# One-hots of a second batch on ScalarE, 0.2 t by a second broadcast, later negatives of x, and bent rows in other pieces, in a graph-attention kernel on one core

## What is computed

```python
HW = h @ W
s = HW @ a[:OUT_F, 0];  t = HW @ a[OUT_F:, 0]
e = leaky_relu(s[row] + t[col], negative_slope=0.2)
m = segment_max(e, row);  ex = exp(e - m[row])
att = ex / segment_sum(ex, row)[row]
agg = segment_sum(att[:, None] * h[col], row)
out = silu(agg) @ base_w.T + einsum('nip,oip->no', b_splines(agg), spline_w)
x = layernorm(x + out)
```

## Time and profile before

| | |
|---|---|
| median of 3 runs | 391.12 us (391.08 to 391.19) |
| the profiled execution's own time | 391.19 us |
| its span in the profile | 389.4 us |
| PE busy | 374.6 us (96%) |
| VectorE busy | 342.1 us (88%) |
| ScalarE busy | 254.7 us (65%) |
| granted TensorE clock, mean | 0.999 |

### The profile page before, as it was taken

One profiled execution on the slowest core, in us unless ns is written; L12 is line 12 of the kernel. 1 busy time (PEld: TensorE's weight loads), 2 busy tenths in 40 slices (PEclk: granted clock), 3 DMA queues, 4 the chain that ended last, 5 costly groups with the idle time before them and its releaser, 6 DMA issues.

```text
span 389.4 us, 5102 instructions
## 1 busy us (share of the span) xinstructions
PE 374.6 (96%) x1915; PEld 299.1 (77%) x1915; DVE 342.1 (88%) x428; ACT 254.7 (65%) x248; POOL 35.9 (9%) x89
## 2 busy tenths in 40 slices
PE   6899889999999999999999999999999999999994
PEld 3556557888888888788888888888888888888883
DVE  8999999987775698999899999889999899989255
ACT  6879643454446979784878764868668686865222
POOL 6001210000000010010100101010010101001000
PEclk9999999999999999999999999999999999999999
DMA  7905970000000055368565553724332554723202
GB/s 253 397 16 125 204 220 2 1 0 2 0 2 0 2 186 193 113 187 267 163 166 158 147 174 120 209 55 108 109 96 66 158 160 116 248 69 99 66 27 101
DMA packets 23634, 46.56 MB, mean 120 GB/s; under 512 B 1882, under 2 KB 2098, under 8 KB 23610
## 3 DMA queue, kind: packets, MB, share of 16 engines
q0 software_dynamic: 12400, 24.00, 24.0%
q1 hardware_dynamic: 11210, 22.25, 17.2%
HBM read 43.67 MB, written 2.57 MB: 119 GB/s over the span
## 4 chain that ended last, share of the span: by engine, by line
PE 85%; DVE 11%; issue 2%; POOL 1%; DVEq 0%; ACT 0%; POOLq 0%
PE PS L1269 63%; PE PS L1212 18%; DVE oh L450 5%; DVE still L464 3%; PE PS L1194 3%; PE PS L1222 1%; DVE scrap L624 0%; DVE ex L640 0%; ACT ex L952 0%; DVE st L832 0%; DVE xr L827 0%; DVEq L247 0%; DVE xr L848 0%; DVE mk L501 0%; DVE C L672 0%
## 5 line engine op out<-in xcount | busy, mean ns | idle before, releaser
L1269 PE MATMUL PS<-wh,s 128*128 128x512 f32 x720 | 223.0, 390 | 0.4 <-issue 0.4
L1269 PEld LDWEIGHTS PS<-wh,s 128*128 128x128 f32 x720 | 135.1, 188 | 29.8 <-issue 1.9
L1269 PE MATMUL PS<-wl,s 128*128 128x512 f32 x360 | 140.1, 389 | 0.0
L1269 PEld LDWEIGHTS PS<-wl,s 128*128 128x128 f32 x360 | 67.6, 188 | 14.0
L1008 ACT ACTIVATE s<-v 128x1280 fp32r<-128x1280 f32 (+1 forms) x32 | 40.0, 1251 | 41.9 <-DVE v L810 23.4
L991 ACT ACTIVATE v<-xt,bias 128x1280 f32<-128x1280 f32 (+1 forms) x32 | 42.9, 1340 | 18.9 <-DVE s L820 17.6
L804 DVE SCALAR_TENSOR_TENSOR v<-v,v 128x1280 f32<-128x1280 f32 (+1 forms) x32 | 46.4, 1451 | 6.3 <-ACT v L994 6.3
L810 DVE SCALAR_TENSOR_TENSOR v<-v,v 128x1280 f32<-128x1280 f32 (+1 forms) x32 | 46.7, 1461 | 3.7 <-DVE v L806 0.5
L820 DVE SCALAR_TENSOR_TENSOR s<-v,s 128x1280 fp32r<-128x1280 f32 (+1 forms) x32 | 46.5, 1454 | 3.3 <-ACT s L1008 3.3
L439 POOL DMA_DIRECT2D wh<-in_splT x32 | 23.0, 717 | 269.9 <-PE PS L1269 172.0
L806 DVE SCALAR_TENSOR_TENSOR v<-v,v 128x1280 f32<-128x1280 f32 (+1 forms) x32 | 46.5, 1453 | 0.0
(11 more groups left out here) (148 smaller groups left out, 332.5 us busy)
## 6 DMA issues: line engine op xcount, KB each, us to landing
wh<-in_splT POOLq DMA_DIRECT2D x32, 512.0 KB, 4.1
wring<-in_splT SPq DMA_DIRECT2D x21, 512.0 KB, 3.9
xt<-in_xT SPq DMA_DIRECT2D x1, 2500.0 KB, 11.9
xh<-in_x POOLq DMA_DIRECT2D x1, 2304.0 KB, 12.3
out<-xr SPq DMA_DIRECT2D x9, 256.0 KB
wh<-in_baseT POOLq DMA_DIRECT2D x4, 512.0 KB, 5.4
xl<-in_x POOLq DMA_DIRECT2D x1, 1536.0 KB, 11.8
wring<-in_baseT SPq DMA_DIRECT2D x3, 512.0 KB, 4.6
```

The lines of the kernel that those rows point to most:

```text
L1269: m = e.matmul(PS[:, w % 8, :], sx[:, ic, tl * 128:tl * 128 + 128], wx[:, ic, :], start=first and n == 0, stop=last and n == 2)
```

## The change

1. Batch 12's `oh` is made by ScalarE: two absolute differences (of 2*REACH[12] = 316 columns) after the copies of each of batches 4 to 7, into two arrays of their own, and a relu over four tiles (1264 columns) after batches 8 and 9. VectorE skips that comparison but keeps its wait for the ring.
2. `st_rows` also writes 0.2 times the rows; SP stores both rows and issues a second broadcast (to `gentle`) behind the first. ScalarE's multiplication at L1024 is gone.
3. The negatives of x are at batches 8 to 17 instead of 6 to 15.
4. `most_along` and what follows it on VectorE come one batch earlier.
5. `bent` of row block 0 has three pieces (0 to 512, 512 to 880, 880 to 1250); the first moves into the middle of the loop body, the second is at its end. The first 500 columns of row block 1's `bent` stand ahead of `weigh(0, 0)`, the other 750 at the old place.

```diff
-BY_SCALAR = 3
+BY_SCALAR, BY_TOO = 3, 12
-HALF = 512
+HALF, NEXT, BEGUN = 512, 880, 500
-        ENDS_AT, MOST_AT, SIZES_AT = 6, 9, NB - 1
-        NEGATIVE_AT = {6 + k: k for k in range(NT)}
+        ENDS_AT, MOST_AT, SIZES_AT = 6, 8, NB - 1
+        NEGATIVE_AT = {8 + k: k for k in range(NT)}
+        DIFFERENCES_AT, ONES_AT = (4, 5, 6, 7), (8, 9)
...
-            e.wait_ge(s_srow, 1)
+            e.wait_ge(s_srow, 2)
             for k, (lo, hi) in enumerate(TCH):
-                e.dma_start(t_row[0:1, lo:hi], strow[32 * k + 1:32 * k + 2, 0:hi - lo]).then_inc(s_tline, 16)
+                e.dma_start(t_row[:, lo:hi].unsqueeze(0), strow[32 * k + 1:32 * k + 2, :, 0:hi - lo]).then_inc(s_tline, 16)
             e.wait_ge(s_tline, 64)
             e.dma_start(trow[:, :], t_row[0:1, :].partition_broadcast(128)).then_inc(s_trow, 16)
+            e.dma_start(gentle[:, :], t_row[1:2, 0:N].partition_broadcast(128)).then_inc(s_gentle, 16)
...
             def moving(b):
-                if b == BY_SCALAR:
+                if b >= RB:
+                    e.wait_ge(s_ct, done(b - RB))
+                if b in (BY_SCALAR, BY_TOO):
                     return
                 h = REACH[b]
-                if b >= RB:
-                    e.wait_ge(s_ct, done(b - RB))
...
-                if b == ENDS_AT + 3:
+                if b == ENDS_AT + 2:
                     most_of_tiles()
...
                     marks(MARKED, ND, 0, NEAR).then_inc(s_near, 1)
+                    bent(0, 0, HALF).then_inc(s_first, 1)
                     e.wait_ge(s_early, n + 1)
...
                     e.tensor_tensor(top[:, 0:LW], trow[:, d], Z[:, 0, d], ALU.subtract).then_inc(s_touch, 1)
-                    bent(0, 0).then_inc(s_first, 1)
+                    bent(0, HALF, NEXT).then_inc(s_next, 1)
...
             greatest(0)
             small(0)
-            bent(0, 1).then_inc(s_z, 1)
+            e.wait_ge(s_next, left)
+            bent(0, NEXT, N).then_inc(s_z, 1)
+            bent(1, 0, BEGUN).then_inc(s_begun, 1)
             weigh(0, 0)
             weigh(0, 1)
             greatest(1)
-            bent(1).then_inc(s_z, 1)
+            e.wait_ge(s_begun, 1)
+            bent(1, BEGUN, N).then_inc(s_z, 1)
...
+            def differences(t):
+                h = REACH[BY_TOO]
+                return e.activation(off_too[t // 4][:, t % 4, :], im[:, MV // 2 - h:MV // 2 + h], ACT.Abs,
+                                    bias=mk_by[:, 1, t:t + 1], scale=-1.0).then_inc(s_off, 1)
+            def ones_of(part):
+                h, k = REACH[BY_TOO], TB // 2
+                e.wait_ge(s_ct, done(BY_TOO - RB))
+                e.wait_ge(s_off, 2 + k * part + k)
+                e.activation(oh[:, BY_TOO % RB, part * k:part * k + k, 0:2 * h], off_too[part][:, :, :], ACT.Relu, bias=1.0,
+                             scale=-1.0).then_inc(s_by, 1)
             def st_rows():
                 e.wait_ge(s_sr, 1)
-                e.copy(strow[0:98, :], PS[0:98, 6, 0:384]).then_inc(s_srow, 1)
+                e.copy(strow[0:98, 0, :], PS[0:98, 6, 0:384]).then_inc(s_srow, 1)
+                e.mul(strow[0:98, 1, :], PS[0:98, 6, 0:384], SLOPE).then_inc(s_srow, 1)
...
+                if b in DIFFERENCES_AT:
+                    differences(2 * DIFFERENCES_AT.index(b))
+                    differences(2 * DIFFERENCES_AT.index(b) + 1)
+                if b in ONES_AT:
+                    ones_of(ONES_AT.index(b))
...
-            e.wait_ge(s_trow, 16)
-            e.mul(gentle[:, :], trow[:, 0:N], SLOPE).then_inc(s_gentle, 1)
...
+                elif b == BY_TOO:
+                    e.wait_ge(s_by, 4)
                 else:
-                    e.wait_ge(s_mv, b + (b < BY_SCALAR))
+                    e.wait_ge(s_mv, b + 1 - (b > BY_SCALAR) - (b > BY_TOO))
```

More of the change, by code:

```diff
@@ L164, in build @@
         dn = at("dn", 33, [128, 2, 128], I32)
+        off_too = [at(f"off{k}", 34 + k, [128, TB // 2, 2 * REACH[BY_TOO]], F16) for k in range(2)]
         war = at("war", 33, [128, 128], F32, 2048)
-        strow = at("strow", 32, [128, 384])
+        strow = at("strow", 32, [128, 2, 384])
         left_col, left_sq, left_in, reach_col = (at(f"left{k}", 36, [128, NCP], F32, 704 * k) for k in range(4))
@@ L193, in build @@
         s_setup = sem("s_setup")
-        (s_reach, s_bits, s_col, s_mk, s_bound, s_left, s_tab, s_mv, s_head, s_ovk, s_ovm, s_ovs, s_ova, s_ovz, s_marked, s_early, s_near, s_touch, s_first, s_late, s_tmax, s_small, s_z, s_p, s_den, s_rden, s_plo,
+        (s_reach, s_bits, s_col, s_mk, s_bound, s_left, s_tab, s_mv, s_head, s_ovk, s_ovm, s_ovs, s_ova, s_ovz, s_marked, s_early, s_near, s_touch, s_first, s_next, s_begun, s_late, s_tmax, s_small, s_z, s_p, s_den, s_rden, s_plo,
          s_a3, s_b3, s_spl, s_slo, s_wlo, s_res, s_bns, s_bna, s_rstd, s_nb, s_fin) = (
             sem(f"v_{n}") for n in (
-                "reach", "bits", "col", "mk", "bound", "left", "tab", "mv", "head", "ovk", "ovm", "ovs", "ova", "ovz", "marked", "early", "near", "touch", "first", "late", "tmax", "small", "z", "p", "den", "rden", "plo",
+                "reach", "bits", "col", "mk", "bound", "left", "tab", "mv", "head", "ovk", "ovm", "ovs", "ova", "ovz", "marked", "early", "near", "touch", "first", "next", "begun", "late", "tmax", "small", "z", "p", "den", "rden", "plo",
                 "a3", "b3", "spl", "slo", "wlo", "res", "bns", "bna", "rstd", "nb", "fin"))
@@ L630, in marks, with bent @@
                 return e.tensor_scalar(Z[:, j0:j1, d], C[:, j0:j1, d], 0.0, BIG, ALU.is_equal, ALU.mult)
-            def bent(j, p=0):
-                lo, hi = pieces(j)[p]
+            def bent(j, lo, hi):
                 if j >= 3:
@@ L764, in _ @@
             greatest(2)
-            bent(2).then_inc(s_z, 1)
+            bent(2, 0, N).then_inc(s_z, 1)
             small(2)
@@ L772, in _ @@
             greatest(3)
-            bent(3).then_inc(s_z, 1)
+            bent(3, 0, N).then_inc(s_z, 1)
             small(3)
@@ L779, in _ @@
             inverse(3)
-            bent(4).then_inc(s_z, 1)
+            bent(4, 0, N).then_inc(s_z, 1)
             greatest(5)
@@ L785, in _ @@
                 if j + 3 < NT:
-                    bent(j + 3).then_inc(s_z, 1)
+                    bent(j + 3, 0, N).then_inc(s_z, 1)
                 if j + 2 < NT:
@@ L887, in moving_by_scalar @@
                 e.wait_ge(s_mk, 1)
-                e.copy(mk_by[:, :], mk[:, TB * b:TB * b + TB, 0]).then_inc(s_by_mk, 1)
+                apart = TB * (BY_TOO - b)
+                e.copy(mk_by[:, :, :], mk[:, TB * b:TB * b + 2 * apart, 0].rearrange("p (a k) -> p a k", a=2)[:, :, 0:TB]
+                       ).then_inc(s_by_mk, 1)
                 e.wait_ge(s_by_mk, 1)
@@ L894, in moving_by_scalar @@
                         m = e.activation(off[:, t, :], im[:, MV // 2 - h:MV // 2 + h], ACT.Abs,
-                                         bias=mk_by[:, part * k + t:part * k + t + 1], scale=-1.0)
+                                         bias=mk_by[:, 0, part * k + t:part * k + t + 1], scale=-1.0)
                     m.then_inc(s_off, 1)
```

8 lines of the change are left out of this document (4 added, 4 removed).

## The result

The changed kernel takes 392.69 us, median of 6 runs (392.55 to 393.43), beside 391.15 us (391.08 to 391.23) for the kernel before on the same chip: ratio 1.0044, 95% interval 1.0033 to 1.0056. It is slower, by 1.5 us; the forecast was 390.1 us, and its range ended at 391.7 us.

A forecast was written before the change was run, and what follows sets the result against it. VectorE's pace, then a short VectorE and ScalarE chain, bounds the kernel before 53.59 us, TensorE afterwards. Terms of -1.22 us plus 0.2 us for xl's wait gave -1.0 us, so 390.1 us, range 389.6 to 391.7.

The forecast's parts named there:

- The views and the bound: Whole kernel: before 53.59 us each microsecond won moves the end, if nothing holds TensorE afterwards; cheaper work behind wins nothing.
- Part 1: Batch 12's one-hot comparison leaves VectorE and TensorE can follow: -1.39 us.
- Part 2: ScalarE's bill for batch 12 and the second row copy: 6.7 us more work, cost 0, bound +0.4 us.
- the eight differences fit into the waits: ScalarE up to the pair copied at 22.82 us: batch 12's added differences cost only idle time.
- Part 3: 0.2 t by DMA through a second broadcast on SP's queue: cost 0, with 6 us of cover before VectorE's need.
- Part 4: VectorE's bent in pieces: +0.35 us in the loop, -0.08 at its end, -0.10 after small.
- Part 5: Negatives of x two batches later delay GpSimd's adding loads of xl, using up 5.6 us of slack: +0.2 us wait.
- When the stream starts: GpSimd's first adding load of xl is issued at 37.4 us, 4.5 us later than before.
- How long it runs: Adding stream moves by 4.5 us to land at 54.2, or 53.5 with up to 0.7 us back from a gone broadcast.
- The weights: SP's 1.05 MB of wring, issued with about 3 us of adding stream left, should not hold xl: 0.
- turn by turn: Rival, 15%: wring and xl packets alternate between two queues, adding 1.7 us to xl's landing; likeliest 391.3 us.
- the clock: TensorE ahead of the sums: a wait of a microsecond or two would not lower its granted clock; no chance assigned.

The follow-up runs named there:

- o_no12: Batch 12's comparison back on VectorE, against the changed kernel with row block 0's xl products last (389.37 us): 389.86 us, 0.9966 of the kernel before.
- o_most9: MOST_AT 9 again (most_along one batch later), against the changed kernel with row block 0's xl products last (389.37 us): 388.49 us, 0.9933 of the kernel before.
- x_gact: Changed kernel without the second broadcast: ScalarE computes gentle from trow again, bent in its old pieces; 393.72 us, 1.0058 of the kernel before.
- x_neg6: Changed kernel with the negatives of x back at batches 6 to 15, xl products at their old place; 395.83 us, 1.0124 of the kernel before.
- o_bent_back: bent back in its old pieces, against the changed kernel with row block 0's xl products last (389.37 us): 389.48 us, 0.996 of the kernel before.
- x_warm: Changed kernel with thirteen products with nought filling TensorE's wait ahead of the xl products; 392.51 us, 1.0032 of the kernel before.
- the control: Changed kernel with only two more register operations on VectorE, which all variants hold; 393.69 us, 1.0072 of the kernel before.
- b_neg8: The kernel before with only the negatives of x moved two batches later, to start at batch 8; 391.20 us, 0.9999 of the kernel before.
- x_loads_again: Changed kernel with SyncE's and GpSimd's first weight loads both waiting for all of xl, run once more for a second profile; 391.08 us, one run.
- x_wring_after_xl: Changed kernel with only SyncE's wring loads waiting for xl, GpSimd's wh load still released by tmax; 391.18 us, 1.0003 of the kernel before.

## Why the prediction was wrong

**The views and the bound** were right: before 53.59 us a microsecond is a microsecond, provided nothing holds TensorE after it. That proviso failed.

**Part 1 (-1.39)** was right for the front. The still of batch 20 came at 42.90 us for 44.97, 2.07 earlier, and at 44.30 in `o_no12`, so part 1 by itself is worth 1.40. The other 0.67 are luck: an idle 0.58 us ahead of batch 19's comparison that I had not priced. In the chain of before a load of a register from `r_size` (2.2 us) stands ahead of it. Without part 1 that load still took 2.5 us, but the earlier `MOST_AT` started it 1.8 us sooner and the idle time was gone (`o_no12`); with part 1 and the old `MOST_AT` it took 0.84 us and the idle time was gone too (`o_most9`). Either is enough. Why the load is short with part 1 was not found.

**Part 2 (0, bound +0.4)**: the prices were a little high (from start to start a difference of 316 columns takes 0.45 us and a relu 1.15, for 0.48 and 1.25), and there was no wait from 23 to 44 us. The step "the eight differences fit into the waits" was right only for an early start. They used up all of ScalarE's idle time after the second pair of copies, and a late start of it is no longer absorbed: a wait of VectorE's of 0.25 us in the profiled execution, and of 0 to 1.18 us over the variants. That is beyond the bound of 0.4, and no term of the sum had it.

**Part 3 (0)**: right in its price; `x_gact` found none for the second broadcast. The landings were 2 us later than reckoned, `trow` 34.61 + 4.2 = 38.8 us for 36.7 and `gentle` 40.4 for 38.4, with cover enough. I had not seen that the two broadcasts stand in the way of an earlier adding stream, which `x_neg6` shows.

**Part 4 (+0.35, -0.08, -0.10)**: right, +0.34, -0.16 and -0.11 by the same distances in the two traces. `o_bent_back` cannot tell its 0.1 us from noise. Sum of parts 1 to 4: forecast -1.22, measured -1.76: -2.07 for the stills, +0.25 for the wait at the marks and +0.07 for part 4, to 0.01.

**Part 5** is the step that failed. *When the stream starts* was right (37.50 for 37.4). *How long it runs* was one sample taken for a constant: I took the 16.8 us of one trace, or up to 0.7 less, and streams alone take 16.8 to 18.4. The 0.7 rested on "that is gone", said of a broadcast ahead of the stream, and it was not gone: SyncE's queue still moved 58 packets in 39 to 40 us, when the stream had its first. *The weights*: I read the 163 packets to 18 as "the load that came first was served nearly alone" and set this to 0. That held until past 52 us and then no longer: the queues shared, and it cost 1.2 to 1.6 us. The trace of before had it one microsecond further on, while the last 0.14 MB of GpSimd's load were still to come. Its queues in 190 to 191 us:

```profile
q1 hardware_dynamic: 149, 0.31, 82.5%
q0 software_dynamic: 52, 0.09, 27.8%
```

The rival "turn by turn" (15%) had the mechanism, with 1.7 us for it, but from the moment of the issue; by the Trainium skill (DMA: Bandwidth & Descriptors, Queues, rings and completion order) the engines alternate packet by packet, and from 53 us on the trace agrees, 75 to 82; from 51 to 52 us it does not, 98 to none.

And the rival's own sum, 391.3 us, was still 1.4 short, because of *the clock*. I wrote that a wait of a microsecond or two "does not frighten me", from a stretch in which TensorE was busy for 0.69 of a microsecond. The wait was 2.81 us of full idleness, the clock went to 1.2 GHz, and 1.7 us were lost on top of it: 6.44 us for twenty products that take 4.84 in `x_warm`, where TensorE was kept busy. The time of `x_warm` is 1.2 us below the control's.

So the slack of 5.6 us that part 5 used "to the microsecond" was spent from three sides: the stream 4.6 us later, its reader 1.8 us earlier through the gain itself, the transfer beside it 1.6 us earlier through that same gain. The first, 3.6 us of it, is free alone, by `b_neg8`; the other two were not tried without it.

## What to carry to other kernels

A gain at the front brings forward whatever it releases: ask of each transfer that it triggers which other one is still under way, and whose reader is now earlier too. Idle time that is filled with moved work no longer absorbs a late start, as on ScalarE here: with the `xl` products last, the three kernels with part 1 scatter by 0.8 to 1.3 us and the one without it by 0.06. Slack that a forecast uses up entirely is a risk on one side only, since a wait of a few microseconds on TensorE also costs its clock; put the work that needs the late operand last, as here, where this order gives 389.37 us, 0.9945 (0.9932 to 0.9958) of the kernel before, and with `MOST_AT` at 9 388.49, 0.9933 (0.9919 to 0.9946), the lowest median, which the intervals do not tell apart. And two queues seen 163 to 18 in one microsecond say who came first, not who will be served next: read the microseconds after it as well.

## What the runs showed of the hardware that was not expected

SyncE's load got its first packets between 3.5 and 4.5 us after its issue (48.50 us, 52 to 53 us) while GpSimd's adding stream was saturated, and an equal share from 53 us on. With no other queue busy such a load had its first packets some 1 us after its issue (before: issued at 50.15 us, first packets in 51.0 to 51.25; `x_loads_again`: 55.90, 56.75 to 57), and no later beside GpSimd's plain loads (`x_wring_after_xl`: 54.82, 55.75 to 56, with GpSimd's queue at 94.6% in 55 to 56). The adding stream moves 0.20 MB per microsecond with its 16 engines full (116.3% by the queue's row), plain loads twice that (397 GB/s).

Ahead of the products of `xl`, TensorE's granted clock fell to 0.50 with idle times of 4.22 (`x_neg6`), 3.33 (`x_gact`), 2.81, 2.42 and 2.33 us and stayed at 1.00 with 1.39, 1.27 and 0.93 us. With 2.33 us it was still 1.00 for the first four products behind the wait (1.20 us) and fell only then. In the control single executions differ by 4 us, the slowest (396.51 us) with the lowest mean clock, 0.988, the fastest (392.19) with the highest, 0.999. The two variants of the kernel before, in which TensorE waits for no DMA there, repeat within 0.6 us (390.73 to 391.16 and 390.81 to 391.39).

GpSimd's `tensor_scalar` over 512 columns took 4.6 us beside VectorE's 16-bit one-hots and 1.9 us beside its 32-bit work on the rows. VectorE's comparison kept its 1.47 us in the first case; in the second its `weigh` over 512 and 738 columns took 1.55 and 1.76 us for 0.69 and 0.93. A few of its operations over four elements or fewer took 0.56 us for 0.14 or 0.15 already beside the first six. The Trainium skill (SBUF — State Buffer, SBUF: two separate sides) has the two engines share one pair of ports as a lock held for a whole instruction, the loser waiting, among other cases when VectorE's operation has two inputs in SBUF, as the comparison and `weigh` have; the lengthened operations on both sides agree with that, though no run here shows the lock itself.
